# A first pair of expert weights copied inside the attention loop, and two divisions moved behind later copies

## The reference, cut to what matters

```python
h = jnp.concatenate([tokenizer(x), txt], axis=1)          # 64 x 82 x 256 (in the attention 16 heads of 16)
h = h + attn(layernorm(h))
h = h + ffn(layernorm(h))

# attn
scores = jnp.einsum('bhqd,bhkd->bhqk', q, k) * scale
attn = jax.nn.softmax(scores + bias, axis=-1)
out = jnp.einsum('bhqk,bhkd->bhqd', attn, v)
return out.reshape(b, t, dim) @ w_out + b_out

# ffn: 2048 tokens, each sent to 2 of 8 experts; entries are sorted by expert
for e in range(8):                                        # rank 64, 1024 hidden columns
    h = gelu(xr @ w1A[e].T @ w1B[e], approximate=False)
    ye = h @ w2A[e].T @ w2B[e]
    out = out + mask * ye
y = zeros.at[tok].add(flat_w[order][:, None] * out)
```

## Time and profile before

| what | value |
|---|---|
| median of 3 runs | 599.6 us |
| profiled execution, its own time | 596.89 us |
| its span (first to last instruction) | 595.0 us |
| TensorE busy in the span | 545.7 us, 92% |
| VectorE busy | 477.2 us, 80% |
| ScalarE busy | 367.1 us, 62% |
| GpSimd busy | 314.5 us, 53% |
| chain that ended last, by engine | PE 60%, DVE 20%, issue 8%, DMA 5%, ACT 4% |

### The profile page before, as it was taken

How to read it: one execution, slowest core, us unless ns; L and a number is a source line. 1 busy time by engine, 2 the same in 40 slices (tenths; PEclk the granted TensorE clock), 3 DMA queues, 4 the chain that set the end, 5 groups by cost and what they waited for, 6 DMA issues and landing times.

```text
span 595.0 us, 20410 instructions
## 1 busy us (share of the span) xinstructions
PE 545.7 (92%) x7904; PEld 456.3 (77%) x7904; DVE 477.2 (80%) x967; ACT 367.1 (62%) x793; POOL 314.5 (53%) x401
## 2 busy tenths in 40 slices
PE   9999989989999999999999999999998799999940
PEld 7788867767788778877888788888886678888830
DVE  3666868898999899999999889998887756666617
ACT  1232234156676677777777677677778667777724
POOL 1577773436746688888888524443121244444430
PEclk9999999989999999999999999999999999999975
DMA  8999301422332334666666644333254354545349
GB/s 280 399 326 333 103 10 43 137 76 82 103 87 87 115 125 134 186 200 199 206 206 194 188 137 148 96 119 124 87 144 139 84 131 107 114 117 114 68 140 327
DMA packets 78185, 89.49 MB, mean 150 GB/s; under 512 B 33550, under 2 KB 58638, under 8 KB 77580
## 3 DMA queue, kind: packets, MB, share of 16 engines
q1 hardware_dynamic: 73340, 78.20, 42.9%
q0 software_dynamic: 4464, 9.35, 5.1%
q10 hardware_dynamic: 288, 0.66, 0.3%
HBM read 48.82 MB, written 36.29 MB: 143 GB/s over the span
## 4 chain that ended last, share of the span: by engine, by line
PE 60%; DVE 20%; issue 8%; DMA 5%; ACT 4%; SPq 1%; POOL 1%; DVEq 0%; POOLq 0%; ACTq 0%
PE banks L1452 8%; PE banks L1418 7%; PE banks L1562 7%; PE banks L1464 6%; DVE mx L1846 6%; PE banks L1577 6%; PE banks L1430 5%; PE banks L1476 4%; PE banks L283 3%; PE banks L1443 3%; DVE prob L1848 3%; DVE qk_space L1834 2%; PE banks L323 2%; ACT probT L1685 2%; PE banks L1547 2%
## 5 line engine op out<-in xcount | busy, mean ns | idle before, releaser
L1685 ACT ACTIVATE probT<-banks 82x328 f32<-82x328 f32 x256 | 109.1, 434 | 9.6 <-PE banks L1452 9.3
L1848 DVE TENSOR_TENSOR prob<-banks,mx 82x656 f32<-82x656 f32 x128 | 107.1, 837 | 4.4
L1452 PE MATMUL banks<-ident_all,prob 82*82 82x82 f32 x1024 | 109.6, 237 | 1.1 <-ACT early L1665 0.9
L1452 PEld LDWEIGHTS banks<-ident_all,prob 82*82 82x82 f32 x1024 | 88.1, 120 | 28.2 <-issue 6.7
L1846 DVE TENSOR_REDUCE mx<-banks 82x8 f32<-82x656 f32 x128 | 104.3, 815 | 5.2 <-PE banks L1443 4.0
L1677 ACT ACTIVATE prob<-prob 82x656 f32<-82x656 f32 x128 | 95.5, 746 | 15.8 <-DVE prob L1848 15.1
L1418 PE MATMUL banks<-hT,wqkv 128*128 128x328 f32 (+10 forms) x320 | 80.6, 385 | 0.0
L1296 POOL TENSOR_TENSOR big<-big,gwq 128x256 f32<-128x256 f32 x41 | 30.2, 738 | 88.0 <-ACT gwq L1672 87.5
L1357 POOL DMA_INDIRECT entry_rows<-cwT,slot_entry x39 | 39.7, 1018 | 63.1 <-ACT cwT L1730 57.3
L1665 ACT ACTIVATE early<-banks 128x328 f32<-128x328 f32 x64 | 28.5, 445 | 56.8 <-PE banks L1464 43.8
L1443 PE MATMUL banks<-qk_space 32*82 32x82 f32 x2048 | 53.0, 240 | 7.4 <-DVE prob L1848 5.7
(11 more groups left out here) (275 smaller groups left out, 1011.3 us busy)
## 6 DMA issues: line engine op xcount, KB each, us to landing
vv<-value_rows SPq DMA_DIRECT2D x57, 192.0 KB
value_rows<-vs SPq DMA_DIRECT2D x41, 256.0 KB, 2.9
share<-shares SPq DMA_DIRECT2D x64, 82.0 KB
slot_rows<-xh SPq DMA_DIRECT2D x1, 4992.0 KB, 33.0
fused_rows<-in_txt SPq DMA_DIRECT2D x1, 4928.0 KB
big<-in_patches SPq DMA_DIRECT2D x2, 1600.0 KB, 12.3
out<-big SPq DMA_DIRECT2D x25, 128.0 KB
big<-entry_rows SPq DMA_DIRECT2D x6, 512.0 KB, 6.5
```

The source lines that it names most:

```text
L1452: mm = te.transpose(bank(("turn", 4 * b + g))[0:T, s * T:s * T + T], prob[:, b % 2, g, s, :], ident_all[0:T, 0:T])
L1685: act.activation(probT[:, b % 2, g, :, :].rearrange("p s t -> p (s t)"), bank(("turn", 4 * b + g))[0:T, 0:4 * T], ACT.Copy).then_inc(S["pr ...
L1848: v.tensor_tensor(prob[:, b % 2, 2 * half:2 * half + 2, :, :], s4, mx[:, half, :, :].unsqueeze(3).to_broadcast([T, 2, 4, T]), ALU.subtract ...
```

## The change

The place of `wb` moves by 64 columns, to the start of the key half, so that the first buffer of `wa` and of `wb` lies within the first regions of the query and key columns. The weights of pair 0 are then copied inside the attention loop: registers and `wa` at the end of period 59, the two pieces of `wb` for the first tile at the end of period 60, those for the second at the end of period 61. After the loop VectorE goes on with pair 1. `divide(30)` and `invert(31)` move behind the `wa` copies of pair 2, `divide(31)` behind those of pair 3. No instruction is added or removed.

```diff
-    wb = qk_flat[:, 4 * 640:8 * 640].rearrange("p (r c) -> p r c", r=2)
+    wb = qk_flat[:, 8 * QT:8 * QT + 4 * 640].rearrange("p (r c) -> p r c", r=2)
...
+        def wide_half(p, h, e):
+            for part in range(2):
+                ins = v.tensor_copy(wb[RANK * h:RANK * h + RANK, p % 2, 640 * part:640 * part + 640],
+                                    WB[RANK * part:RANK * part + RANK, bass.ds(e, 1), :].rearrange("p a c -> p (a c)"))
+            return ins
+
         def own_wb(p, owners):
             if p >= 2:
                 v.wait_ge(S["y_ps"], p - 1)
             for h, e in enumerate(owners):
-                for part in range(2):
-                    ins = v.tensor_copy(wb[RANK * h:RANK * h + RANK, p % 2, 640 * part:640 * part + 640],
-                                        WB[RANK * part:RANK * part + RANK, bass.ds(e, 1), :].rearrange("p a c -> p (a c)"))
+                ins = wide_half(p, h, e)
             ins.then_inc(S["wb_ready"], 1)
...
-            if b == NB - 1:
+            if b == NB - 5:
                 v.wait_ge(S["f_w_in"], 32 * NE)
                 owners[0] = experts(0)
                 own_wa(0, owners[0])
+            if b == NB - 4:
+                wide_half(0, 0, owners[0][0])
+            if b == NB - 3:
+                wide_half(0, 1, owners[0][1]).then_inc(S["wb_ready"], 1)
             if b >= 5 and b % 2 == 1:
                 divide(b // 2 - 2)
-        own_wb(0, owners[0])
-        invert(NB // 2 - 2)
         owners[1] = experts(1)
         own_wa(1, owners[1])
+        invert(NB // 2 - 2)
         owners[2] = experts(2)
         own_wb(1, owners[1])
-        divide(NB // 2 - 2)
         copy_t2(0)
-        invert(NB // 2 - 1)
         for p in range(1, NPAIR):
             if p + 1 < NPAIR:
                 own_wa(p + 1, owners[p + 1])
+                if p == 1:
+                    divide(NB // 2 - 2)
+                    invert(NB // 2 - 1)
+                if p == 2:
+                    divide(NB // 2 - 1)
                 if p + 2 < NPAIR:
                     owners[p + 2] = experts(p + 2)
                 own_wb(p + 1, owners[p + 1])
             copy_t2(p)
-            if p == 1:
-                divide(NB // 2 - 1)
```

## The result

The changed kernel takes 596.22 us (median of 22 runs) against 599.02 us (22 runs of the kernel before beside it). The medians differ by 2.8 us; the ratio measured for the pair is 0.9943, interval 0.9924 to 0.9962, which is 3.4 us won (2.3 to 4.6). Forecast were 2.1 us and a time of 597.5 (596.2 to 599.5). The sign came as forecast; the gain is larger, and the time lies at the very edge of the range. Means and slopes in this text count only executions within 1.5% of the fastest of their kernel in a comparison. Over all of them the means are 599.1 us (before, 145 runs) and 596.7 us (changed, 46 runs), so the best figure is 2.4 us, 1.7 to 3.1 at 95%. That holds the 2.1, but it is made of other parts.

A forecast was written before the change was run, and what follows sets the result against it. No engine is full in late attention, where a VectorE-TensorE loop sets the periods; VectorE bounds the handover, TensorE the steady experts. 2.0 + 0.62 + 0.65 = 3.27 won, 1.15 lost: 2.1 us, so 597.5 us, range 596.2 to 599.5.

The forecast's parts named there:

- The delay in the periods: Attention periods 59 to 61: inserted copies delay the attention's end by 0.95 + 0.2 + 0 = 1.15 us; bounds 0.4 to 2.6.
- The rival in which GpSimd is met in full: Periods 59 to 61: copies collide with GpSimd wherever it works, delay 2.1 to 2.6 us, time 598.4 to 598.9; chance 0.16.
- The rival of copies paid in full: Periods 59 to 61: each copy delays the next shift by its length, 5.0 us, so 1.7 lost, 601.3; chance 0.06.
- that of the least delay: Periods 59 to 61: no copy meets a GpSimd addition, delay only 0.4 us, time 596.7; chance 0.10.
- The handover: Attention's end to first expert pair: without copies ahead of `divide(29)`, `hidden(0)` and `down(0)` come 2.0 us earlier; 0.4 to 2.4.
- The rival of a handover that stays: Late shares or ScalarE's list hold `down(0)`; only 0.4 of the 2.0 us comes, 0.5 won, 599.1; chance 0.13.
- The order: First expert pairs: `wa` copies of pairs 2 and 3 ahead of waiting divisions save 0.62 and 0.65 us before `low(2)` and `low(3)`.
- The room behind `divide(31)`: Projections of tiles 39 and 40 and pair 3's `wb` have 2.0 and 1.5 us to spare, so queuing there costs nothing.
- a shift that I keep: Whole run: the median's 2.7 us above the profiled execution was carried over unchanged, giving 599.6 - 2.1 = 597.5 us.

The follow-up runs named there:

- order alone: Kernel before with only the last two divisions and last inversion moved behind the copies of pairs 2 and 3, pair 0's copies left in place: 0.9984.
- division first: Kernel before with `divide(29)` put ahead of the registers and `wa` copies of period 63, nothing copied early: 0.9985.
- longer wait: Kernel before with the four `wb` copies of pair 0 made twice, the first set for nothing: 601.73 us, 1.0062.
- the copies alone: Kernel before with pair 0's copies moved into periods 59 to 61, divisions and inversions after the loop in the old order: 0.9976.
- the copies spread and the matmuls added: Changed kernel with registers in period 57, pair 0's copies over periods 59 to 62, and ten unread matmuls in TensorE's gaps: 0.9944 against the kernel before.
- the added matmuls: Unread identity matmuls in TensorE's gaps: 10 in the changed kernel, 0.9963; 15 in the kernel before, 1.0005; both against the kernel before.
- spreading the copies: Changed kernel with registers in period 57, one `wa` copy each in 59 and 60, two `wb` each in 61 and 62: 0.9948 and 0.9968 against the kernel before.

## Why the steps of the prediction came and its sum did not

**The delay in the periods: right beside an execution whose shares come in time.** 1.16 for 1.15; by period 0.98, 0.22 and -0.03 for 0.95, 0.2 and 0. The registers showed 0.83 of issue for 0.90, and the copies 1.30, 1.42 and 0.99. The rival in which GpSimd is met in full (2.1 to 2.6) did not come, though the copies of periods 59 and 60 were longer than the 0.81 of the earlier trace rows, and two GpSimd additions beside the second took 2.01 where they took 1.42. The Trainium skill, page SBUF — State Buffer, section "SBUF: two separate sides", says that of a GpSimd operation and such a copy the one that starts first keeps the shared port for its whole instruction and the other waits; that both sides lost time in period 60, 0.43 for the copies (two `wb` copies alone took 0.99 in period 61, more than the 0.81 that the prediction took as the least) and 0.59 for the additions, agrees with it in kind. The rival of copies paid in full, with its 5.0, fell too, and so did that of the least delay, which was nearest in time (596.7): copies did meet GpSimd.

**The handover: right where TensorE ran at full clock on both sides.** Without a stretch `down(0)` follows the last shift's end by 7.19 in place of 9.30: 2.1 for 2.0. The steps were as put: the division at the shift's end, `copy_sums(62)` behind the weighing, no gap of TensorE, GELU at once behind the table load. There the Trainium skill, page ScalarE: Activation LUTs, section "What ACT_TABLE_LOAD costs", would have added a drain of some 1.38 us to the 1.28 of the load; in the execution without a stretch the load ends at 468.30 and the GELU begins at 468.32, so the trace shows no such drain here. The rival of a handover that stays fell.

**The order: right, a little low without a stretch.** 16.71 became 15.3, 1.4 for 1.27; where a stretch had already covered the wait ahead of `low(2)` (16.02), 0.7. The room behind `divide(31)` was real but thin (the 0.99 and 0.98 above).

**What failed: the sum.** All its terms came from one execution, and two of them do not hold from one execution to the next.

The first is "a shift that I keep". The 2.7 us between the profiled execution and the median were carried over unchanged, as if no part of them lay in the stretch that the change touches. The shift is not kept. The time at 1.2 GHz was 25.0 us in the profiled execution of the kernel before (clock 0.979, span 595.0), 30.9 in its 123 runs with a clock on record, and 28.3 in the 46 of the changed kernel. Across the runs of all ten kernels a microsecond more at 1.2 GHz goes with 0.38 us more of span (0.02 standard error, one slope with a level for each kernel). By that slope 5.9 us more go with 2.3 of the shift of 2.7, and in the changed kernel 3.3 x 0.38 = 1.3 are left of it. The forecast with that shift would have been 594.8 + 1.3 = 596.1 us; measured were 596.2 in the first comparison and 596.7 over all runs. That it comes so near is in part luck, since the 594.8 holds the whole 2.1.

The second is the 1.15 lost in the periods, read beside an execution in which period 61 took 4.89. The kernel before often loses time there by itself: in its four profiles and the three of kernels that leave these periods alone (order alone, division first, longer wait) period 61 took 4.89, 4.86, 6.32, 6.73, 6.96, 5.50 and 4.88. With the copies in periods 59 to 61 (the changed kernel, and the copies alone) it took 4.85 to 4.86 in four profiles and 5.30 in one. So over the four periods the changed kernel is 0.3 us late on average of the four profiles each (20.22 against 19.88), and not 1.15. Whether the copies keep the shares from coming late, or five executions were lucky, is open; with the copies spread and the matmuls added they did come late once (6.32).

Averaged over the four profiles of each kernel the parts are then 2.0 won in the handover, 0.9 by the order and 0.3 lost in the periods, 2.5 in all, near the 2.4 over all runs, though four profiles a kernel leave an error of about 1.3. In single executions the parts scatter: by the schedule alone it is 0.8 + 0.7 - 1.16 = 0.3 with 6.8 us at 1.2 GHz on both sides, since such a stretch covers the waits anyway, and 2.1 + 1.4 - 1.16 = 2.3 without one. Beside the 1.27 and the 1.15 of the forecast the order gave less on average and the delay took less; the two errors work against each other, which is why the 2.1 lay near.

How far this is shown: the time at 1.2 GHz does differ between the two kernels, 2.6 us by the clocks of 123 and 46 runs (standard errors 0.4 and 0.6 us). What makes it differ is not shown. One reading is TensorE's shorter wait in the handover: making the copies twice raised the time at 1.2 GHz (3.4 with 1.7), and the four profiles of each put the difference between 440 and 480 us (7.7 and 4.3 us on average). The other is the late shares of period 61: the slow time of the two largest figures, 10.2 and 13.6, began behind them and ahead of the handover, and where the shares came in time the stretches are alike (0 and 6.9 before; 0, 3.4, 6.8 and 6.8 changed). No run takes the late shares away and leaves the handover as it was. At equal time at 1.2 GHz the regression leaves the changed kernel 1.3 us shorter (0.22 standard error), and 2.6 us less at 1.2 GHz go with 1.0; but the slope is a correlation over runs, late shares lengthen the span and may bring on the slow stretch as well, and the added matmuls, which lowered the time at 1.2 GHz by an edit, won nothing. So the split of the gain between schedule, clock and late shares stays open. The first comparison's 3.4 is partly a matter of its runs, as two more gave 1.7.

## What to carry to other kernels

Terms read from one execution hold for that execution: before a term or a shift is kept, look at several profiles of the kernel before, at the granted clock in the stretch that changes and at the waits for DMA ahead of it. Where two waits stand one behind the other, taking out the first alone gains nothing (5.95 for 5.97), so trace each of them to the work that ends it. A hole in a loop of two engines took about its own length of other work for nothing here, but work moved behind a DMA wait lives on that DMA's worst latency, not on the one seen (2.29 in one execution, 3.71 in another).

## What the runs showed that was not expected

- Stretches at 1.2 GHz lay at different places: between 18 and 22, 55 and 62, 130 and 134, and 462 and 478 us, in one execution and not in the next; only the last 24 us had one in every profile. A TensorE busy only 0.59 of 2 us ahead of the handover (changed kernel, no stretch) was followed by full clock, and one busy 1.39 of 2 us (profile after) by 6.8 us at half.
- The last shares came 6.7 us behind the start of their reciprocal in one execution of the changed kernel and 8.0 in another: the wait for them was 2.29 and 3.54 us. SyncE issued `spread_shares` 1.75 us behind `send_shares` in the first and 3.30 in the second, so most of the difference lies in that first transfer.
- A transfer that had been in time can come late in a new order: the 0.64 for the denominators, which took back most of what spreading the copies had won.
- The shares of period 61 came late in two of four profiles of the kernel before, which made period 61 longer by 1.4 and 1.8 us.
